# The third tile's transposition of softmax weights one loop step later in a graph-attention, mix-attention and fast-feedforward layer on one core

## The reference, cut to what matters

```python
# mix attention, per head
weighted_dots = dots * spiky_weights[:, :, :, None]
weights = softmax(weighted_dots, axis=-1)
out = einsum('bhij,bhjd->bhid', weights, v)
# GNN attention, per head (mask from the edges)
attn = softmax(scores * scale + mask[None], axis=-1)
out = einsum('hnm,hmd->hnd', attn, v2)
```

## Time and profile before

| what | value |
|---|---|
| median of 3 runs | 722.76 us (722.17 to 723.04) |
| the profiled execution's own time | 722.35 us |
| its span, first to last instruction | 720.6 us |
| PE busy / PEld busy | 700.5 us (97%) / 667.4 us (93%) |
| DVE / ACT / POOL busy | 476.7 (66%) / 402.4 (56%) / 233.6 us (32%) |
| granted PE clock | 0.999 of full speed |
| line L1807 (gemm_T) on the chain that ended last | 37% of the span |
| line L1832 (gemm_N) / L1871 (head_T's transpositions) on it | 12% / 4% |

### The profile page before, as it was taken

One profiled execution on the slowest core, in us unless ns is written; L12 is line 12 of the kernel. 1 busy time (PEld: TensorE's weight loads), 2 busy tenths in 40 slices (PEclk: granted clock), 3 DMA queues, 4 the chain that ended last, 5 costly groups with the idle time before them and its releaser, 6 DMA issues.

```text
span 720.6 us, 11750 instructions
## 1 busy us (share of the span) xinstructions
PE 700.5 (97%) x4490; PEld 667.4 (93%) x4490; DVE 476.7 (66%) x960; ACT 402.4 (56%) x695; POOL 233.6 (32%) x212
## 2 busy tenths in 40 slices
PE   3999999999999999999999999999999998999998
PEld 3989999999999999999999999998899998989896
DVE  6758874875678467776666566657677456877644
ACT  4555556564565555668587675422433346777441
POOL 4734232232332323126122264662004521322240
PEclk9999999999999999999999999999999999999999
DMA  5421635413223133231312242333135758897352
GB/s 214 163 105 60 233 135 217 177 61 121 90 87 118 61 116 113 96 117 60 117 60 74 90 188 88 129 122 116 60 117 170 245 188 350 307 410 268 146 160 89
DMA packets 21910, 105.15 MB, mean 146 GB/s; under 512 B 5840, under 2 KB 6224, under 8 KB 13056
## 3 DMA queue, kind: packets, MB, share of 16 engines
q1 hardware_dynamic: 12880, 80.84, 30.5%
q0 software_dynamic: 8688, 23.42, 9.3%
q10 hardware_dynamic: 288, 0.14, 0.1%
HBM read 92.71 MB, written 18.06 MB: 154 GB/s over the span
## 4 chain that ended last, share of the span: by engine, by line
PE 85%; DVE 7%; ACT 4%; DMA 2%; issue 2%; POOL 0%; POOLq 0%; DVEq 0%; ACTq 0%
PE g_bank L1807 37%; PE g_bank L1832 12%; PE o_bank L1882 4%; PE t_bank L1871 4%; PE s_bank L2185 2%; PE s_bank L1859 2%; PE s_bank L1860 2%; DVE w_lo L1166 2%; PE t_bank L2185 2%; PE g_bank L1761 1%; PE s_bank L2395 1%; PE s_bank L2393 1%; PE s_bank L2394 1%; PE t_bank L2286 1%; DMA raw<-wstream_dram 1%
## 5 line engine op out<-in xcount | busy, mean ns | idle before, releaser
L1807 PE MATMUL g_bank<-act_hi,w_hi 128*128 128x384 f32 x488 | 170.0, 348 | 0.0
L1807 PE MATMUL g_bank<-act_hi,w_lo 128*128 128x384 f32 x488 | 163.7, 335 | 0.0
L1807 PE MATMUL g_bank<-act_lo,w_hi 128*128 128x384 f32 x488 | 163.4, 335 | 0.0
L1166 DVE TENSOR_TENSOR w_lo<-raw,w_hi 128x2048 fp32r<-128x2048 f32 x58 | 137.1, 2364 | 36.2 <-ACT w_hi L697 34.2
L697 ACT ACTIVATE w_hi<-raw 128x2048 fp32r<-128x2048 f32 x67 | 128.1, 1912 | 30.4 <-PE s_bank L2185 12.5
L494 POOL DMA_INDIRECT edge_table<-ew,eidx x51 | 67.3, 1319 | 162.3 <-DMA edge_table<-ew,eidx 157.9
L1807 PEld LDWEIGHTS g_bank<-act_hi,w_hi 128*128 128x128 f32 x488 | 91.8, 188 | 2.7 <-issue 2.6
L1807 PEld LDWEIGHTS g_bank<-act_lo,w_hi 128*128 128x128 f32 x488 | 91.9, 188 | 0.0
L1807 PEld LDWEIGHTS g_bank<-act_hi,w_lo 128*128 128x128 f32 x488 | 91.6, 188 | 0.0
L441 POOL TENSOR_TENSOR w_lo<-raw,w_hi 128x2048 fp32r<-128x2048 f32 x10 | 46.9, 4694 | 103.4 <-ACT w_hi L697 97.1
L1303 DVE TENSOR_TENSOR pT_lo<-t_bank,pT_hi 128x384 fp32r<-128x384 f32 x96 | 50.6, 554 | 33.7 <-ACT pT_hi L790 33.3
(11 more groups left out here) (326 smaller groups left out, 1645.9 us busy)
## 6 DMA issues: line engine op xcount, KB each, us to landing
raw<-wstream_dram SPq DMA_DIRECT2D x68, 1024.0 KB, 4.9
xg<-xs POOLq DMA_DIRECT2D x12, 512.0 KB, 8.3
ys<-y_ring POOLq DMA_DIRECT2D x6, 512.0 KB, 8.8
yv<-y_ring POOLq DMA_DIRECT2D x12, 256.0 KB, 2.3
x_sb<-x_dram SPq DMA_DIRECT2D x3, 512.0 KB, 5.2
y_acc<-x_dram POOLq DMA_DIRECT2D x3, 512.0 KB, 5.1
out_dram<-out_sb SPq DMA_DIRECT2D x6, 256.0 KB, 2.0
edge_table<-ew,eidx POOLq DMA_INDIRECT x51, 2.6
```

What stands on the lines that cost most here:

```text
L1166: V.tensor_tensor(flat(w_lo[to][:, :, :]), raws[raw_slot(n.base)], flat(w_hi[to][:, :, :]), ALU.subtract) \
L1807: last = mm(out, w2[a], x2[b], start=k == 0 and a + b == 0, stop=not after and k == KT - 1 and a == 1)
```

## The change

Tile 2's transposition is issued one k step later: in the last head of every mix group after k = 4 instead of k = 3 of m = 0; in the second GNN head of groups 0 to 2 after (1,1) instead of (1,0); in the output product after (1,6) instead of (1,5). No instruction is added or removed, and the order on ACT, DVE, POOL and SP is the same.

```diff
-                            if k == 3:
+                            if k == (4 if h == HG - 1 else 3):
                                 head_T("mix", g, h, tile, (2,))
...
-                    if (m, k) == (1, 0):
+                    if (m, k) == (1, 1):
                         T(1, 2)
...
-                    if (t, k) == (1, 5):
+                    if (t, k) == (1, 6):
                         T(1, 2)
```

## The result

The change makes the kernel slower. Over 20 runs of each the median went from 723.21 us (722.17 to 724.64) to 725.12 us (724.20 to 732.09), ratio 1.0032 with a 95% interval of 1.0023 to 1.0042. The medians differ by 1.91 and 1.64 us. The ratios say 2.3 and 1.7 us: they go with the mean, and in the first measurement two runs of 728.29 and 732.09 us draw it up. So the change costs 1.6 to 2.3 us, where 1.0 was forecast, and 725.12 lies above the range of 722.2 to 724.8. One execution of the kernel before beside e1 to e4 took 868.98 us at a mean granted clock of 0.756, and is left out of every number here.

The account below looks back on a forecast made before the run. PE, busy 97% of the span, was taken as the bound, so moves pay only where it waits. +0.07 - 0.45 + 1.39 + 0 gave +1.0 us on 722.76, so 723.8 us, range 722.2 to 724.8.

Parts of the forecast that it names:

- Mix groups 0 to 2: Last mix heads: the wait removed at tile 2 returns at hidden_layer, gain handed back whole; +0.07 us for the three.
- Mix group 3: Last mix head: PE 0.52 us ahead, restart costs 0.07, gain kept if DVE's split starts before POOL's subtraction; -0.45 us.
- Rival 1: DVE's L1166 after the last mix head: POOL keeps the port, -0.45 gone; 724.2 us, or 724.4 with full GNN delay; chance 0.22.
- Second GNN heads: Groups 0 to 2: transposition without a wait delays ACT and DVE; 0.35 + 0.52 + 0.52 = +1.39 us.
- Output product: Tile 2 there: DVE takes it late anyway, so the 0.35 us step is covered; 0 us.
- the term for everything behind the output product: Stages from there to the end: all hang on PE, nothing absorbs the shift; no cost of their own in the sum.
- The base: Whole kernel: forecast median of the kernel before, 722.76 us, to which the +1.0 us was added.

Follow-up runs that it names:

- e1: Against the kernel before, only the second GNN heads of groups 0 to 2 have tile 2's transposition one k step later; 726.03 us against 723.11, ratio 1.0036.
- e4: e3 plus, in GNN groups 0 to 2, head 2's tile 2 transposition and its product one k step later; 721.00 us against 723.11, ratio 0.9969.
- e3: e2 plus hidden_layer of the last mix head one k step later; 722.77 us, ratio 0.9987 to the kernel before.
- e9: e1 plus head 2's tile 2 transposition and its product one k step later in the GNN heads; one run, 723.35 us beside 723.03.
- e6: Against the kernel before, only the output product's tile 2 transposition one step later; one run, 723.49 us beside 723.40.
- e8: The changed kernel measured again beside the kernel before on one chip; 725.04 us against 723.40, ratio 1.0023.
- e5: e1 with the GNN heads' tile 2 transposition two k steps later instead of one; 726.10 us against 723.40, ratio 1.0037.
- e2: Against the kernel before, only the mix heads have tile 2's transposition one k step later; 722.96 us against 723.11, ratio 0.9998.
- e10: e4 plus head 2's tile 2 transposition and its product two steps later in the output product's second unit; 719.91 us against 723.03, ratio 0.9968.

## Why the prediction was wrong, point by point

1. **Mix groups 0 to 2: right.** Forecast a new wait at hidden_layer and +0.07 us in all; measured +0.10, and e3 shows that this wait is what takes the gain.
2. **Mix group 3: right.** Forecast -0.45, with the split ahead of POOL's; measured -0.49 at the first GNN scores (from +0.10 to -0.39) and -0.41 behind the restart there, and the two durations changed places. The order rested on 0.23 us and on two errors of 0.14 that cancelled, so there was luck in it. Rival 1 didn't come about; that the time ended beyond its 724.4 has another cause (point 5).
3. **Second GNN heads: right in mechanism, a little low.** Forecast +1.39, measured +0.62, +0.48 and +0.46, 1.56 us, of which 0.08 in group 0 is the restart at the first GNN scores that belongs to point 2. The term that was mis-sized is group 0, set at 0.35 in the hope that DVE's gap of 0.46 us ahead of scale_pair would shrink; it stayed 0.46, and 0.54 was paid (0.53 in e1). That half of each step is lost at the scores, forecast as 0.26, holds (0.27 in group 1, and e9).
4. **Output product: right**, 0.01 (e6).
5. **The step that failed** is the term for everything behind the output product, which the sum had at nothing: "From these places to the end all stages hang on PE, so I expect nothing to absorb it." The prediction shows no row of that stretch. Nothing was absorbed, as it says: the sum up to there, forecast as +1.0, was +1.16 and stands at +1.15 at 592.91. But the medians differ by 1.91 and, in e8, by 1.64, so what came behind it is 0.75 us, or 0.4 in e8, whose profile has +1.23 there. PE waits 2 us there behind a streamed unit, and whether the granted clock halves after that wait differs from execution to execution. By the mean clocks the changed kernel has it in 24 of 30 runs, the kernel before in 16 of 54. At the 0.3 to 0.7 us between runs with and without it within a kernel that is worth (0.80 - 0.30) x 0.5 = 0.25 us, at the 1.2 us by which profiles with it exceed those without between 592.91 and 623.60 (+1.2 to +1.5, against -0.35 to +0.6) it is some 0.6.
6. **The base** was low too: 722.76 was the median of three runs, 723.21 that of twenty. Of the 1.3 us between 723.8 and 725.12 that is 0.45, and the heads' 0.16 and the 0.75 behind them make up the rest, to rounding. Counted from 723.21 the same range would have ended at 725.25, above what was measured.

What stays open: 1.16 + 0.25 to 0.6 makes 1.4 to 1.8 us, well inside e8's interval (0.9 to 2.3 us) and at the lower end of the first measurement's (1.7 to 3.0). On e8's chip the account nearly closes: 1.3 to 1.5 us like with like, of which 1.23 are the heads', and 0.1 to 0.2 for 7 of 10 runs against 5 of 15; but the groups without the halved clock are of 3 and 10 runs. If the difference is nearer 2 us, a part of it has no name here. No run set the halved clock on or off by itself, and why it comes more often in some kernels isn't settled either. Beside how late PE is at 592.91, it came in 1 of 5 (e5, +3.2), 4 of 5 (e1, +1.5), 24 of 30 (after, +1.2), 16 of 54 (before), 2 of 11 (e2, -0.3), 8 of 11 (e3, -1.4), 3 of 7 (e4, -2.6) and 5 of 12 (e10, -3.2), with no order in it. That it follows from where in time the 2 us wait falls is a guess that no run tested.

## What to carry to other kernels

Move a step later only where it waits now, and before doing so list who is in line behind it on the engines that consume it. Where it doesn't wait and that line has no slack, one step of delay is paid in full (e1, e5); where the line has slack, it costs nothing (e6); and where the line touches the next wait, the gain is only handed on (e2). Moving that next waiter along (e3), leaving the transpositions that don't wait in place and moving others that do (e4, e10) made a kernel 3.1 us faster than before, where the change made it 1.6 to 1.9 slower. And a stretch in which nothing is changed still needs its rows read, and its scatter, before it is put at nothing.

## What the runs showed of the hardware that was not expected

- The granted clock may halve for 3.4 us behind a wait of 2 us on PE, in some executions of one and the same kernel and not in others (the means of e8's ten runs are 0.997 to 1.000); products of 256 columns then start every 0.21 us instead of 0.12.
- The shared port acts as the Trainium skill has it (SBUF — State Buffer, "SBUF: two separate sides": whoever starts first keeps it, the other is blocked). This case's rows agree, the order decided by 0.23 us either way: DVE 3.78 and POOL 1.85 us with POOL first, DVE 2.29 and POOL 3.77 with DVE first.
- Up to 592.91 the two profiles of the changed kernel place each PE instruction within 0.1 us of each other, so single profiles tell effects of 0.3 us (0.05%) that the time of a run can't.
